# A flamingo block on one core: the two expert passes with row transposes, first products and second transposes two pairs apart, and loop bodies of twenty pairs

## The reference

```python
x = x + tanh(g_xattn) * cross_attention(layernorm(x), ctx_768)     # 8 heads of 64, 77 context tokens
x = x + tanh(g_ffn) * moe(layernorm(x))

# moe, xf: 8192 x 256, E = 16 experts, hidden width 128, two experts a token
scores = softmax(xf @ Wg.T); wk, idx = top_k(scores, 2)
h = u * silu(g)   with  u, g = split(xf @ W1[e])                   # W1[e]: 256 x 256
z = sum over the two chosen experts of  wk * (h @ W2[e])           # W2[e]: 128 x 256
ys = (u * silu(g) of xf @ Ws1) @ Ws2                               # shared expert
return z + ys
```

## Time and profile before

| | us |
|---|---|
| median of 3 runs | 1073.16 (1066.94 to 1075.34) |
| the profiled execution | 1074.5 |
| its span, first to last instruction | 1072.2 |

### The profile page before, as it was taken

The page is one execution under the profiler, slowest core; times in us unless marked ns, Lnnn a source line. Parts: engine busy times, 40 slices in busy tenths (PEclk is TensorE's granted clock), DMA queues, the critical chain, the costliest instruction groups (busy, mean ns, idle before and its releaser), DMA issues. The chain is left out here.

```text
span 1072.2 us, 21198 instructions
## 1 busy us (share of the span) xinstructions
PE 948.8 (88%) x6828; PEld 873.8 (81%) x6829; DVE 797.3 (74%) x1824; ACT 471.7 (44%) x967; POOL 505.9 (47%) x635
## 2 busy tenths in 40 slices
PE   3799999999999999997799999978887877878883
PEld 3699999999999999987588888865877775877772
DVE  5699899999999998885588888881565552655552
ACT  4456555555555555542644554430333231323331
POOL 7546354544545353441235555551455553354554
PEclk9799999999999999998799999999999999999997
DMA  8213332222323221221524444456899963766650
GB/s 219 69 44 97 86 97 85 72 71 83 97 86 97 86 61 41 63 56 55 174 90 168 168 157 175 149 208 206 286 296 318 300 235 112 236 189 215 199 172 13
DMA packets 108328, 150.96 MB, mean 141 GB/s; under 512 B 21831, under 2 KB 72395, under 8 KB 108241
## 3 DMA queue, kind: packets, MB, share of 16 engines
q1 hardware_dynamic: 92880, 107.60, 33.6%
q0 software_dynamic: 15360, 42.24, 10.5%
HBM read 90.19 MB, written 65.90 MB: 146 GB/s over the span
## 5 line engine op out<-in xcount | busy, mean ns | idle before, releaser
L652 POOL TENSOR_TENSOR prob<-prob,row_sum 128x616 f32<-128x616 f32 x64 | 77.9, 1217 | 132.6 <-DVE row_sum L853 132.2
L75 PE MATMUL ps_h<-w_flat,eyT_hi 128*128 x320 | 98.3, 307 | 36.0 <-DVE eyT_lo L1610 33.0
L1491 POOL DMA_INDIRECT rows_scratch<-prow x80 | 78.7, 984 | 91.5 <-DVE prow L1628 73.1
L1491 POOL DMA_INDIRECT out<-prow x80 | 78.7, 983 | 85.5 <-DVE prow L1628 63.9
L1585 ACT ACTIVATE eyT_hi<-ps_ey 128x512 fp32r<-128x512 f32 x80 | 48.3, 604 | 139.4 <-PE ps_ey L1513 100.5
L1080 POOL DMA_INDIRECT rows_scratch<-row,slot x64 | 67.9, 1061 | 75.5 <-DVE row L1329 60.9
L1628 DVE TENSOR_TENSOR prow<-ps_z,prow 128x512 f32<-128x512 f32 x80 | 54.9, 687 | 65.0 <-PE ps_z L77 37.1
L75 PEld LDWEIGHTS ps_h<-w_flat,eyT_hi 128*128 128x128 f32 x320 | 62.0, 194 | 43.1 <-issue 43.1
L76 PE MATMUL ps_h<-w_flat,eyT_hi 128*128 x320 | 90.9, 284 | 0.0
L77 PE MATMUL ps_h<-w_flat,eyT_lo 128*128 x320 | 90.5, 283 | 0.0
L1610 DVE TENSOR_TENSOR eyT_lo<-ps_ey,eyT_hi 128x512 fp32r<-128x512 f32 x80 | 55.1, 688 | 42.3 <-ACT eyT_hi L1585 36.5
(11 more groups left out here) (267 smaller groups left out, 3410.5 us busy)
## 6 DMA issues: line engine op xcount, KB each, us to landing
prow<-rows_scratch SPq DMA_DIRECT2D x160, 258.0 KB
rows_scratch<-blank SPq DMA_DIRECT2D x34, 258.0 KB, 2.9
xT_raw<-in_xT SPq DMA_DIRECT2D x32, 256.0 KB, 4.4
x_tok<-in_x SPq DMA_DIRECT2D x32, 256.0 KB, 3.0
x_scratch<-x_tok SPq DMA_DIRECT2D x32, 256.0 KB, 3.3
row<-x_scratch SPq DMA_DIRECT2D x16, 512.0 KB, 4.0
x_ahead<-in_x SPq DMA_DIRECT2D x26, 256.0 KB, 4.3
w_raw<-in_W SPq DMA_DIRECT2D x16, 256.0 KB
```

Source lines behind the costliest of these rows:

```text
L75: nc.tensor.matmul(out, lh, rh, start=start and n == 0, stop=False)
L652: nc.gpsimd.tensor_tensor(pr, pr, row_sum[i][:, :].unsqueeze(2).broadcast_to((P, H, CK)), ALU.mult).then_inc(normed, 1)
L1491: pool.indirect_dma_start(dram, bass.IndirectOffsetOnAxis(target, 0), row[u][:, i, 0:columns], None, bounds_check=bound, oob_is_err=False) ...
```

## The change

The three kinds of work between transposes and second products get more distance. With `HIDDEN, TURN, DOWN = 2, 4, 5` step s does T of pair s, H of s - 2, A of s - 4 and D of s - 5 on TensorE; ScalarE and VectorE take the same lags. `eyT` and `a` have four buffers (`NB`), `aT` and all PSUM tiles keep two. The `silu` tile goes: ScalarE writes into `a` and VectorE multiplies in place, so ScalarE waits for the second transposes of the pair four before instead of VectorE for those of two before. There are twenty row tiles (`U` = 20), so 20 steps are written out, and the loop body has 20 steps and runs once in each pass; two neighbouring slots share one `scattered` semaphore. The blank rows keep their places in SP's queue. Elsewhere, in `prepare` and `mix`, several semaphores with one use each are merged into counting ones (`weights_hi`, `centred`, `ws_steps`, `tables_ready`), with the counts that belong to the same instructions; one hunk of that stands here for all.

```diff
@@ -357,11 +357,10 @@
-        qmean_done, qmean_scaled, centred = sem("qmean_done"), sem("qmean_scaled"), sem("centred")
-        wk_hi_done, wk_lo_done, wq_hi_done, wq_lo_done = (
-            sem("wk_hi_done"), sem("wk_lo_done"), sem("wq_hi_done"), sem("wq_lo_done"))
+        centred = sem("centred")
+        weights_hi, wk_lo_done, wq_lo_done = sem("weights_hi"), sem("wk_lo_done"), sem("wq_lo_done")
...
@@ -1415,15 +1414,16 @@
-    U = 10
+    U = 20
+    HIDDEN, TURN, DOWN = 2, 4, 5
+    NB = 4
...
-        yT = [[sb(f"eyT{i}_{s}", [P, DC, 2 * P], F32R) for s in ("hi", "lo")] for i in range(2)]
-        silu = [sb(f"silu{i}", [P, 2, HID]) for i in range(2)]
-        a = [sb(f"a{i}", [P, 2, HID]) for i in range(2)]
+        yT = [[sb(f"eyT{i}_{s}", [P, DC, 2 * P], F32R) for s in ("hi", "lo")] for i in range(NB)]
+        a = [sb(f"a{i}", [P, 2, HID]) for i in range(NB)]
...
-        scattered = [sem(f"pscattered{i}") for i in range(U)]
+        scattered = [sem(f"pscattered{i}") for i in range(U // 2)]
...
@@ -1460,7 +1460,7 @@
-                    wait(sp, scattered[u], 32 * (q // U))
+                    wait(sp, scattered[u // 2], 64 * (q // U))
...
-                    first = (q - U) * 4 // 6
-                    if q >= U and (q - U) % 6 == 0 and first < E:
+                    first = (q - 10) * 4 // 6
+                    if q >= 10 and (q - 10) % 6 == 0 and first < E:
                         blank_tails(nc, sp, nc.sync, c, c.rows0, 0, range(first, first + 4), c.blanked0)
...
-                            bounds_check=bound, oob_is_err=False).then_inc(scattered[u], 16)
+                            bounds_check=bound, oob_is_err=False).then_inc(scattered[u // 2], 16)
...
                     def step(s, u, j):
                         if u == 0:
                             known.clear()
-                            if exists(s - 3):
-                                load_weights_at(known, s - 3, -3)
-                        if u % 2 == 0:
-                            load_weights_at(known, s - 1, u - 1)
+                            if exists(s - DOWN):
+                                load_weights_at(known, s - DOWN - 1, -DOWN - 1)
+                                load_weights_at(known, s - TURN, -TURN)
+                        if u % 2 == 0 and exists(s - HIDDEN):
+                            load_weights_at(known, s - HIDDEN, u - HIDDEN)
                         if exists(s):
                             transpose_rows(s, u, j)
-                        if exists(s - 1):
-                            hidden(s - 1, (u - 1) % 2, known[u - 1])
-                        if exists(s - 2):
-                            transpose_a(s - 2, u % 2)
-                        if exists(s - 3):
-                            down(s - 3, (u - 3) % 2, known[u - 3])
-
-                    rounds(pe, step, first, lag=3)
+                        if exists(s - HIDDEN):
+                            hidden(s - HIDDEN, u - HIDDEN, known[u - HIDDEN])
+                        if exists(s - TURN):
+                            transpose_a(s - TURN, u - TURN)
+                        if exists(s - DOWN):
+                            down(s - DOWN, (u - DOWN) % 2, known[u - DOWN])
+
+                    rounds(pe, step, first, lag=DOWN)
...
@@ -1579,22 +1582,22 @@
                         if exists(s):
-                            p = u % 2
+                            p, n = u % 2, u % NB
                             act.wait_ge(yT_done, s + 1)
-                            wait(act, h_done, s - 1)
-                            nc.scalar.activation(yT[p][0][:, :, :], ps_y[p][:, :, :], ACT.Copy).then_inc(yT_hi, 1)
-                        if exists(s - 1):
-                            q, p = s - 1, (u - 1) % 2
+                            wait(act, h_done, s - NB + 1)
+                            nc.scalar.activation(yT[n][0][:, :, :], ps_y[p][:, :, :], ACT.Copy).then_inc(yT_hi, 1)
+                        if exists(s - HIDDEN):
+                            q, p, n = s - HIDDEN, (u - HIDDEN) % 2, (u - HIDDEN) % NB
                             act.wait_ge(h_done, q + 1)
-                            wait(act, a_done, 2 * (q - 1))
-                            nc.scalar.activation(silu[p][:, :, :], ps_h[p][:, :, HID:], ACT.Silu).then_inc(silu_done, 1)
-                        if exists(s - 2):
-                            q, p = s - 2, u % 2
+                            wait(act, aT_done, q - NB + 1)
+                            nc.scalar.activation(a[n][:, :, :], ps_h[p][:, :, HID:], ACT.Silu).then_inc(silu_done, 1)
+                        if exists(s - TURN):
+                            q, p = s - TURN, (u - TURN) % 2
...
@@ -1605,30 +1608,29 @@
                             v.wait_ge(silu_done, q + 1)
-                            wait(v, aT_done, q - 1)
                             for i in range(2):
-                                V.scalar_tensor_tensor(a[p][:, i, :], ps_h[p][:, i, 0:HID],
-                                                       row[b][:, i, weight:weight + 1], silu[p][:, i, :],
+                                V.scalar_tensor_tensor(a[n][:, i, :], ps_h[p][:, i, 0:HID],
+                                                       row[b][:, i, weight:weight + 1], a[n][:, i, :],
                                                        ALU.mult, ALU.mult).then_inc(a_done, 1)
```

More of the change, by code:

```diff
@@ L505, in _ @@
                 v.wait_ge(wq_in, 16)
[L506 to L509, removed]
+                nc.vector.tensor_reduce(qmean[:, :], wq_raw[:, :, :], AX.X, ALU.add).then_inc(centred, 1)
+                v.wait_ge(centred, 1)
+                nc.vector.tensor_scalar(qmean[:, :], qmean[:, :], 1.0 / D, None, ALU.mult).then_inc(centred, 1)
+                v.wait_ge(centred, 2)
                 for q in range(4):
@@ L1168, in _ @@
                 down(STEPS - 1)
-                pe.wait_ge(table_ready, 1)
+                pe.wait_ge(tables_ready, 2)
                 for n, column in enumerate((1, 0, 3, 2)):
@@ L1214, in _ @@
                 act.wait_ge(wg_in, 16)
-                nc.scalar.activation(wg[:, :, 0:E], wg_raw[:, :, :], ACT.Copy).then_inc(wg_hi, 1)
+                nc.scalar.activation(wg[:, :, 0:E], wg_raw[:, :, :], ACT.Copy).then_inc(ws_steps, 1)
                 act.wait_ge(root_ready, 1)
@@ L1360, in tables @@
                     V.scalar_tensor_tensor(table[:, CHOICES:], by_choice(passed)[:, :, E - 1], float(SLOT_ROWS),
-                                           table[:, CHOICES:], ALU.mult, ALU.add).then_inc(table_ready, 1)
+                                           table[:, CHOICES:], ALU.mult, ALU.add).then_inc(tables_ready, 1)
                     link(V.memset(c.weights_at[:, :], 0))
@@ L1474, in _ @@
                     load(c.rows1, q)
-                    first = (q - U) * 4 // 6
-                    if q >= U and (q - U) % 6 == 0 and first < E:
+                    first = (q - 10) * 4 // 6
+                    if q >= 10 and (q - 10) % 6 == 0 and first < E:
                         blank_tails(nc, sp, nc.sync, c, c.rows0, 0, range(first, first + 4), c.blanked0)
-                for u in range(U):
-                    sp.wait_ge(scattered[u], 32 * ROUNDS)
+                for pair in scattered:
+                    sp.wait_ge(pair, 64 * ROUNDS)
                 sp.wait_ge(c.blanked0, 16 * E)
@@ L1500, in _ @@
                         send(U * j + u, u, c.out, D, 0, T - 1)
-                for u in range(U):
-                    pool.wait_ge(scattered[u], 64 * ROUNDS)
+                for pair in scattered:
+                    pool.wait_ge(pair, 128 * ROUNDS)
             @block.tensor
@@ L1526, in hidden, with transpose_a @@
                         last = products(nc, ps_h[p][:, i, :], [
-                            (yT[p][0][:, k, token], yT[p][1][:, k, token], *split(at[i], k * D)) for k in range(DC)])
+                            (yT[n][0][:, k, token], yT[n][1][:, k, token], *split(at[i], k * D)) for k in range(DC)])
                     last.then_inc(h_done, 1)
-                def transpose_a(q, p):
+                def transpose_a(q, u):
+                    p, n = u % 2, u % NB
                     pe.wait_ge(a_done, 2 * q + 2)
@@ L1595, in step @@
                             nc.scalar.activation(aT[p][0][:, :, :], ps_a[p][:, 0:2, :], ACT.Copy).then_inc(aT_hi, 1)
-                    rounds(act, step, first, lag=2)
+                    rounds(act, step, first, lag=TURN)
             @block.vector
@@ L1629, in step @@
                                             ALU.add).then_inc(final, 1)
-                    rounds(v, step, first, lag=3)
+                    rounds(v, step, first, lag=DOWN)
 def flamingo(nc, x, xT, ctxT, g_xattn, g_ffn, WqT, Wk, Wv, Wout, bout, WgT, W1, W2, Ws1, Ws2, out, upto=9):
```

65 lines of the change are left out of this document (33 added, 32 removed).

## The result

| | median us | runs | profiled execution, span us | mean granted clock |
|---|---|---|---|---|
| before | 1071.70 | 7 | 1072.2 | 0.968 |
| after | 1083.63 | 7 | 1085.0 | 0.952 |

The ratio after to before is 1.012, with a 95% interval of 1.009 to 1.016. The changed kernel is slower, as forecast, but by 12 us (1.2%) and not by 23.

The account below looks back on a forecast made before the run. TensorE's signals, held about 1.45 us per send, were taken to bound the kernel. Each pass gains 8.7 us of pace and 2.7 of fill, +22.8 together: 1074.5 + 22.8 - 1.3 = 1096 us, range 1040 to 1117.

Parts of the forecast that it names:

- What bounds the kernel: In the passes, TensorE's signals are held while sends run, about 1.45 us per send from the run's start.
- D one step after A stops TensorE, six sends in a run: In the passes, TensorE stops at D for held `aT_lo`; three pairs join one run, 11.6 us if H is held first.
- second rival: No change in the passes: the lock at two pairs and 7.37 us stays, only fill is added, 1079 us; chance 0.22.
- A held first: Case in the passes where A's signal is held first: sends start at 2.3, three pairs take 11.05 us, 3.68 a pair.
- Steady pace: Sends in each pass: 3.86 us a pair over 40 pairs, 154.4 us instead of 145.7, so +8.7 us.
- The row that I averaged over: Kernel before, runs starting at 956.95 and 968.73 with six sends between: three pairs take 11.78 us, 3.93 each.
- Two of the patterns' paces in the sum: Paces per pair in the passes: D and H held first in turn, 3.79 us; H held first with three pairs, 3.85.
- Fill: Start of each pass: first D comes two steps later, costing between 0 and 5.5 us, taken as 2.7.
- Body of twenty and table load at nothing: Loop in `passes`: fewer turns and one table load more at the body's head cost 0.
- Row tiles: Row loads in `passes`: twenty tiles let SP load 20 pairs ahead, bringing nothing and costing 0.
- third rival: Passes slower still, TensorE slower after long idles: 4.36 us a pair, 31.4 us more a pass, 1136 us; chance 0.10.
- faster rival: In the passes, two steps of distance cover the hold: 2.9 us a pair, 1019 us, half of it 1046; chance 0.26.

Follow-up runs that it names:

- experiment 1: Changed kernel with distances back to 1, 2, 3, run twice, signals passing: 1008.69 us, ratio 0.996, and 1009.17 us, ratio 0.997, to the kernel before.
- experiment 8: Kernel before with one send per pair in the second pass: 1004.01 us, ratio 0.991, with signals passing; 1024.77 us, ratio 0.962, with signals held.
- experiment 9: Kernel before with a GpSimd memset of 256 columns, waited for, behind every send, signals held: 1144.89 us, ratio 1.076.
- experiment 6: Changed kernel with its table of weight positions moved by two entries, so loads begin at multiples of 16 bytes, signals held: 1085.94 us, ratio 1.016.
- experiment 7: Kernel before with its table of weight positions moved by two entries, so loads begin 8 bytes past a multiple of 16, signals held: 1079.18 us, ratio 1.009.
- experiment 3: Changed kernel without the weights' table loads (constant addresses), distances 2, 4, 5 kept, signals passing: 1013.90 us, ratio 1.002 to the kernel before.
- experiment 2: Changed kernel with ten row tiles, a body of ten and five buffers, distances 2, 4, 5 kept, signals passing: 1095.87 us, ratio 1.081 to the kernel before.
- experiment 4: Changed kernel run again unaltered, with its trace, signals held: 1084.23 us, ratio 1.014 to the kernel before.
- experiment 5: Kernel before run again unaltered, with its trace, signals held: 1071.82 us.

## Why the prediction was right, and where it was off

- **What bounds the kernel: right.** TensorE's signals held while sends run, 1.45 us for each, counted from the run's start. It was read from starts of consumers alone; the semaphore times show it directly, and experiments 1, 8 and 9 show it by its absence. Some late signals get out earlier, which the reading didn't have. What I did not see is that it is a condition of the run and not of the kernel: the whole prediction is for the held one.
- **D one step after A stops TensorE, six sends in a run: right in kind, too often.** 3.16 us of idle for `aT_lo` and 11.47 us for three pairs (forecast 11.6) are the forecast pattern. But the two profiles of the kernel after have 5 and 8 runs of six or more beside 26 and 21 of four; those of the kernel before have 2 each. The second rival's lock lives on beside it: 12 and 8 intervals of 7.3 to 7.5 us between runs of four, where the profiles of the kernel before have 23 and 24, and five of 8.1 us in each (A held first, which I had put down for runs of six).
- **Steady pace: the term that was mis-sized.** Forecast 3.86 us a pair. From the start of the first send to the end of the last it is 151.1 and 142.6 us in the first profile and 153.4 and 146.0 in the second, 3.71 us a pair on average; the two profiles of the kernel before (145.7 and 146.4, 146.9 and 144.3) give 3.65. So +2.4 us a pass, not +8.7. The row that I averaged over, the 11.78 us of the earlier trace rows, is real but rare. That even the +2.4 comes from the forecast pattern is not shown: in experiment 6, with short table loads, the sends take 147.8 and 144.2 us, the 3.65 us a pair of the kernel before, though it has ten runs of six or more; in experiment 7 long loads alone, with the distances of the kernel before, make it 154.1 and 146.5. The long loads are as good an explanation, each of the two on one profile. (Two of the patterns' paces in the sum are a little low: (10.3 + 8.7)/5 is 3.80 and 11.6/3 is 3.87; the sum would change by under 1 us.)
- **Fill: right in place, too small.** Taken 2.7 us, bound 5.5. Measured from first transposes to first send: +4.4 and +5.2 us in the first pair of profiles, +4.2 and +5.5 in the second, 4.8 on average. The useful work in those steps counted for almost nothing. My reading, not tested by itself: what follows is paced not by TensorE's work but by GpSimd's runs of sends, which start later by two full steps (2 x 2.74 = 5.5). Had I asked who sets the pace afterwards, the upper bound was the value to take. Experiment 3 has the fill without the hold: +4.5 us at the first send and +5.9 us between the passes, though the medians show only 5.2 us for both passes together.
- **Body of twenty and table load at nothing: wrong, unseen.** Behind the last send 1.3 us are lost (7.9 us from the start of the last send to the end before, 9.2 in all six profiles with a body of twenty); nearly all of it is GpSimd's closing DRAIN, 6.59 us instead of 5.29. These six have twenty row tiles too, so which of the two costs it isn't separated. The table load was covered by the row that shows a step with a load and no gap; what I didn't ask is what distance 2 does to the load's address. It makes the load three times as long (0.34 to 1.0 us and more). Its price is shown for the kernel before (8 us, experiment 7), not for the kernel after.
- **Row tiles: right as far as it went.** They bring next to nothing at distances 1, 2, 3 (experiment 1), but where signals pass the change needs them: with ten, TensorE waits 49 us for rows (experiment 2), with twenty 12 (experiment 3).
- **Rivals.** The sum of the parts measured is 9.7 for the fill, 4.9 for the steady state and 1.3 for the end, 15.9 us in the profiles, less 2.3 us that the stretches ahead of and between the passes happened to give back: 13.6, against 13.5 for the mean difference of the two pairs of spans. The time, 1084, lies between the second rival (1079) and the forecast (1096), and nearer to the rival: that it came out clearly slower owes more to the fill (9.7 us, taken as 5.4) and to the end (1.3 us, taken as nothing) than to the steady state that the forecast rested on (4.9 us, taken as 17.4). This part of being right is luck. The third rival is there in part: idles over 2.5 us are 5 in each profile of the kernel after against 2 and 1 before, and granted clocks of 0.94 and 0.90, in experiment 4 of 0.91 and 0.91, against 0.99 and 0.96, in experiment 5 of 0.96 and 0.97; what the lower clock costs wasn't separated. The faster rival didn't come in. The remark of the Trainium skill (Perfetto Trace Analysis, Optimization Strategy) that "consistent bubbles" can mean too little SBUF or PSUM for the next tile would have led to it. With four buffers at the old distances the ratio is 0.996 where signals pass (experiment 1), and where they are held the bubbles only moved in the changed kernel. Here it was something else: the bubble of the earlier trace rows was a late signal.

## What to carry to other kernels

When two engines with nothing else to do resume together, ask which signal they waited for and when its sender had really finished; if that is much earlier, the signal is late, and not the work. Here two steps more of distance and four buffers did not help, and fewer back-to-back sends did (experiment 8). When a pipeline gets longer, charge its fill in full unless the engine that is delayed has slack afterwards; here 4.8 of the 5.5 us came due in each pass. When an index into a table shifts by a step, look at where its loads now begin.

## What was not expected of the hardware

- The same program in the same order took 1011 or 1071 us, the second with TensorE's signals held during runs of indirect sends, the first without; one chip showed both.
- Most held signals are released 1.45 us times the number of sends after the start of the run (5.79 us for four), in the run at 800.97 within 0.4 us of each other; a quarter of the late ones get out earlier, near 2.1, 2.8, 3.6 or 4.3 us. The sends themselves are recorded 1.29 us apart.
- A register load of four entries took 0.34 us by the median from a multiple of 16 bytes behind the table's start, and 1.0 us and more (up to 3.6 us, experiment 7) from 8 bytes past one.
- With a memset and a wait for it between two sends, a send came every 2.27 us on GpSimd: 0.98 for the send, 0.33 for the memset and 0.96 idle, where back-to-back sends leave 0.30 idle.
